# Attention with a routed feed-forward: both expert layers of 12 token tiles go through lists of routed rows, and products are scattered to a row per token and choice

## The chip, the cores and the metric

The kernel runs on one core of a Trainium2 chip. The metric is device time in microseconds of one execution; lower is better. The core has a matrix engine (PE), a vector engine (DVE), a scalar engine (ACT), a general engine (POOL) and a queue engine (SP) that only starts transfers. Each engine works through its own instructions in order and waits on semaphores for the others. Ordinary transfers are started by SP; indirect ones, in which every one of 128 rows has its own address, are started by POOL.

## What is computed

```python
x = x + xattn(_layernorm(x), ctx, ctx, mask, Wq, bq, Wk, bk, Wv, bv, Wo, bo)   # x: 2 x 1024 x 256, 64 keys, 16 heads
x = x + ffn(_layernorm(x), P_w, U1, U2, U3, W1, W2, b2)

def ffn(x, P_w, U1, U2, U3, W1, W2, b2):       # 12 experts, 3 chosen for each token
    xa = xf @ P_w.T
    C1 = _route_combine_weights(xa, U1, 3, 1.0)  # softmax over the top 3, zero elsewhere
    C2 = _route_combine_weights(xa, U2, 3, 1.0)
    C3 = _route_combine_weights(xa, U3, 3, 1.0)
    h = gelu(_mixture(xf, C1, W1))               # sum over experts of C[n,e] * (W[e] @ x[n])
    return _mixture(h, C2, W2) + C3 @ b2         # W1, W2: 12 x 256 x 256
```

## The kernel before

The 2048 tokens are 16 tiles of 128. Products that need float32 precision are three passes over a high and a low part of each operand (`split_product`, L1347): for both halves of the 256 inputs that is six matmuls.

**Attention.** One loop step handles one tile on every engine, with the tiles staggered: `scores` of tile t+1, `transpose_probs` of t, `transpose_a` of t-1, `queries` of t+2, `weigh_values` of t, `output_project` of t-1, `transpose_x` of t+3 on PE. Beside it ACT (L743) and POOL (L509) split one of the 12 chunks of expert weights (a pair of experts each, six per layer) into high and low part.

**Layer 1, dense.** For tiles 0 to 13, PE multiplies the tile with all 12 experts: six pairs of 36 matmuls in all, 512 columns each (`expert_pairs`). DVE adds the products with the routing weights (L1123). The gelu follows on ACT (L784). In the same steps the next tile is routed: logits on PE, `find_top`, `combine_weights` and `rows_of` on DVE, the exponentials as a power on POOL (L574). For tiles 0 to 11 (`S = 12`) ACT then scales h with each of its three layer 2 weights (L792), and POOL writes the three scaled tiles to DRAM with indirect transfers (`send_h`, L595): each row goes to a place in the list of its expert.

**Layer 2, by lists.** The 12 lists are cut into 47 blocks of 128 rows (`BLOCKS`), each of one expert. SP loads a block (`load_block`, L418), PE transposes it (L1649), ACT and DVE split it (L832, L1277), PE multiplies it with its expert's weights, six matmuls of 256 columns, ACT copies the product out (L840) and SP writes it to DRAM (L432). Buffers are rings: 8 loaded blocks, 3 transposed ones, 4 pairs of products. After the last block POOL fetches the three rows of every token with 36 indirect transfers (`fetch_y`, L605), and DVE adds them to x (L1302).

**The dense rest.** Tile 12's layer 2, tiles 14 and 15 in layer 1 and tiles 13 to 15 in layer 2 are dense products (six slots of 36 matmuls), beside which the fetches run. Every order is written out by hand; there is no scheduler.

```python
            def fetch_y(i):

                t, k = FETCH_ORDER[i]
                if i >= FETCHES:
                    pool.wait_ge(y_summed, i - FETCHES + 1)
                if i > AHEAD:
                    pool.wait_ge(pair_done, PAIRS * slot2(S) + i - AHEAD)
                pool.indirect_dma_start(out=y_fetched[i % FETCHES], out_offset=None, in_=y_rows[:, :],
                                        in_offset=bass.IndirectOffsetOnAxis(y_row[:, t, k:k + 1], 0)
                                        ).then_inc(y_back[i % FETCHES], 16)
```

## Time and profile before

| | us |
|---|---|
| Median of 3 timed runs | 366.2 (364.51 to 367.71) |
| Span of the profiled execution | 374.3 |
| PE busy in it | 340.8 (91%) |
| DVE busy | 285.7 (76%) |
| POOL busy | 189.6 (51%) |
| ACT busy | 181.8 (49%) |

The profiled execution gives no other time of its own than its span, which is 8.1 us longer than the median of the timed runs. Busy times of PE count overlapping matmuls generously. The share of an engine over the span says little here, since the program is a row of stages with different limits; the stages have to be read one by one.

### The profile page before, as it was taken

Reading aid. Unit: us, or ns where it says so; the run is one execution under the profiler, and the core shown is the slowest. Engines: PE = TensorE matmul, PEld = TensorE weight load, DVE = VectorE, ACT = ScalarE, POOL = GpSimd, SP = SyncE. Lnnn points to the kernel's source line nnn. Section 1 sums busy time; section 2 is a strip of 40 time slices with the busy share of each in tenths; the row PEclk is TensorE's granted clock in tenths of the full one; section 3 lists DMA queues with packets and bytes.
Section 4 is the critical chain, followed back from the end, with each engine's and each line's share of the span. In section 5 each row is a group of like instructions: output and inputs, shape, how many; then the busy total and the mean of one; then the engine's idle time right before and its main releaser. Section 6 shows DMA issues by size and latency. Waiting matters only on the chain.

```text
span 374.3 us, 7464 instructions
## 1 busy us (share of the span) xinstructions
PE 340.8 (91%) x2079; PEld 293.8 (79%) x2079; DVE 285.7 (76%) x941; ACT 181.8 (49%) x447; POOL 189.6 (51%) x263
## 2 busy tenths in 40 slices
PE   3879999999998979999999999989979899997990
PEld 3669898898998858887888888779969898885770
DVE  3899889898978568988888888886535438748757
ACT  2386978888893153344444444326747660211100
POOL 4447465655755046776666666511201017857760
PEclk9999999999999999999999999999989999998796
DMA  7910113132100001111111111556757742442442
GB/s 209 365 41 4 56 57 109 61 86 82 56 2 15 3 0 42 45 42 42 45 42 45 43 45 43 187 180 185 227 186 242 221 155 82 122 120 71 129 112 98
DMA packets 27129, 36.43 MB, mean 97 GB/s; under 512 B 3572, under 2 KB 21208, under 8 KB 26968
## 3 DMA queue, kind: packets, MB, share of 16 engines
q1 hardware_dynamic: 23080, 26.47, 22.2%
q0 software_dynamic: 3456, 9.44, 8.4%
q8 instruction: 15, 0.25, 0.3%
q10 hardware_dynamic: 560, 0.13, 0.2%
q14 instruction: 18, 0.15, 0.1%
HBM read 21.35 MB, written 14.68 MB: 96 GB/s over the span
## 4 chain that ended last, share of the span: by engine, by line
PE 65%; issue 11%; DVE 9%; ACT 6%; POOL 4%; DMA 3%; SPq 0%; ACTq 0%; DVEq 0%; POOLq 0%
PE banks L1347 48%; DMA stage<-h_rows 2%; PE banks L1649 2%; PE banks L1389 2%; PE banks L1414 2%; PE banks L1399 2%; DVE q_hl L923 2%; PE banks L1402 1%; PE banks L1404 1%; PE banks L1424 1%; ACT w_h L743 1%; PE banks L1473 1%; POOL w_l L509 1%; ACT prob L674 1%; DMA x_all<-in_x_dram 1%
## 5 line engine op out<-in xcount | busy, mean ns | idle before, releaser
L1123 DVE SCALAR_TENSOR_TENSOR sum<-banks,mask_all,sum 128x256 f32<-128x256 f32 x160 | 68.2, 477 | 16.3 <-PE banks L1347 8.2
L1347 PE MATMUL banks<-w_h,h_h 128*128 128x512 f32 x120 | 50.5, 421 | 1.4 <-DVE h_l L1054 1.4
L574 POOL TENSOR_TENSOR top_e<-euler,top_d 128x9 f32<-128x9 f32 x16 | 29.1, 1820 | 38.7 <-DVE top_d L1066 38.7
L1347 PE MATMUL banks<-w_h,xf_h 128*128 128x512 f32 x120 | 48.6, 405 | 0.0
L1347 PE MATMUL banks<-w_l,h_h 128*128 128x512 f32 x120 | 48.0, 400 | 0.0
L1347 PE MATMUL banks<-w_h,h_l 128*128 128x512 f32 x120 | 47.9, 399 | 0.0
L1347 PE MATMUL banks<-w_l,xf_h 128*128 128x512 f32 x120 | 47.0, 392 | 0.0
L1347 PE MATMUL banks<-w_h,xf_l 128*128 128x512 f32 x120 | 46.8, 390 | 0.0
L509 POOL TENSOR_TENSOR w_l<-stage,w_h 128x1024 f32 (+1 forms) x12 | 28.7, 2395 | 31.9 <-ACT w_h L743 31.9
L605 POOL DMA_INDIRECT stage<-y_rows,mask_all x36 | 35.9, 997 | 14.9 <-issue 8.9
L1277 DVE TENSOR_TENSOR kbd_l<-banks,kbd_hh 128x256 fp32r<-128x256 f32 x47 | 19.7, 423 | 23.4 <-ACT kbd_hh L832 23.1
L784 ACT ACTIVATE xn_t<-xn 128x256 f32<-128x256 f32 x16 | 6.7, 417 | 58.0 <-DVE xn L1128 52.8
L1347 PE MATMUL banks<-w_h,kbd_hh 128*128 x94 | 31.1, 331 | 0.5 <-DVE kbd_l L1277 0.5
L1424 PE MATMUL banks<-v_ext,prob_t 128*128 128x34 f32 x256 | 30.0, 273 | 0.0
L1424 PEld LDWEIGHTS banks<-v_ext,prob_t 128*128 128x128 f32 x256 | 29.9, 192 | 0.1
L1123 DVE SCALAR_TENSOR_TENSOR s_d<-banks,mask_all,s_d 128x256 f32<-128x256 f32 x40 | 17.1, 477 | 15.2 <-PE banks L1347 13.1
L595 POOL DMA_INDIRECT h_rows<-prob_t,mask_all x24 | 24.9, 1037 | 6.0 <-issue 6.0
L1347 PEld LDWEIGHTS banks<-w_h,h_h 128*128 128x128 f32 x120 | 23.3, 194 | 5.6 <-DVE h_l L1054 1.6
L1347 PEld LDWEIGHTS banks<-w_l,h_h 128*128 128x128 f32 x120 | 23.2, 194 | 5.4
L1347 PE MATMUL banks<-w_h,kbd_l 128*128 x94 | 26.9, 286 | 0.0
L1347 PE MATMUL banks<-w_l,kbd_hh 128*128 x94 | 26.8, 285 | 0.0
L1347 PEld LDWEIGHTS banks<-w_l,xf_h 128*128 128x128 f32 x120 | 22.5, 188 | 5.3 <-issue 0.3
(194 smaller groups left out, 890.3 us busy)
## 6 DMA issues: line engine op xcount, KB each, us to landing
stage<-in_w_t_dram SPq DMA_DIRECT2D x12, 512.0 KB, 3.7
stage<-h_rows SPq DMA_DIRECT2D x47, 128.0 KB, 2.7
y_rows<-prob SPq DMA_DIRECT2D x12, 256.0 KB, 2.8
y_rows<-stage SPq DMA_DIRECT2D x11, 256.0 KB, 2.9
out_dram<-x_all SPq DMA_DIRECT2D x16, 128.0 KB
h_rows<-wo_sb SPq DMA_DIRECT2D x13, 128.0 KB, 1.7
x_all<-in_x_dram SPq DMA_DIRECT2D x1, 1024.0 KB, 7.8
x_all<-in_x_dram SPq DMA_DIRECT2D x1, 768.0 KB, 7.8
```

Of the source, the lines that this page charges most:

```text
L509: pool.tensor_tensor(w_l[:, n, :, :], stage[:, slot, :, :], w_h[:, n, :, :].bitcast(F32), ALU.subtract).then_inc(w_split, 1)
L574: pool.tensor_tensor(top_e[:, :], euler[:, :], top_d[:, :, :].rearrange("p r k -> p (r k)"), ALU.pow).then_inc(e_ready, 1)
L595: pool.indirect_dma_start(out=h_rows[:, :], out_offset=bass.IndirectOffsetOnAxis(h_row[:, t, k:k + 1], 0), in_=h_w[t % 2][k], in_offset=No ...
L605: pool.indirect_dma_start(out=y_fetched[i % FETCHES], out_offset=None, in_=y_rows[:, :], in_offset=bass.IndirectOffsetOnAxis(y_row[:, t, k ...
L923: ins = dve.tensor_tensor(q_hl[other, :, group, :], q[r, :, :], q_hl[r, :, group, :].bitcast(F32), ALU.subtract)
L1123: dve.scalar_tensor_tensor(out=sums[e % 2][:, :], in0=product, scalar=weights[:, e:e + 1], in1=sums[e % 2][:, :], op0=ALU.mult, op1=ALU.ad ...
L1277: dve.tensor_tensor(bt_l[j % HT], banks[:, j % HT, 0:D].rearrange("p (c t) -> p c t", c=C), bt_h[j % HT].bitcast(F32), ALU.subtract).then_ ...
L1347: ins = pe.matmul(dst, a(c), b(c), start=(i == 0), stop=(i == len(terms) - 1))
L1389: ins = pe.matmul(ps_q[:, m, :], wq_sb[:, c, m * P:(m + 1) * P], xn_t[:, c, :], start=(c == 0), stop=(c == C - 1))
L1399: pe.matmul(banks[:, c, :].rearrange("p (h k) -> p h k", k=KEYS), ident_b[:, :], mask_bias[:, t, :].unsqueeze(1).to_broadcast([P, HPC, KEY ...
L1414: ins = pe.transpose(ps_pt[:, j, :], prob[:, 2 * j:2 * j + 2, :].rearrange("p h k -> p (h k)"), ident[:, :])
L1424: ins = pe.matmul(ps_v[:, j * 2 * VW:(j + 1) * 2 * VW], prob_t[:, j, :], v_ext[:, b, j, :], start=True, stop=True)
```

## The change

S stays 12, but for those tiles both expert layers now go by lists.

- Attention is unrolled (`for t in range(1, T + 1)`). Its steps now also hold, for earlier tiles, the second normalisation (`stats2`, `inverse_deviation2`, `normalise2`), `transpose_xf`, `copy_xf`, `logits`, `copy_z`, and for tiles 0 to 11 layer 1's routing in four groups of 4, 4, 2 and 2 tiles. `normalise2` writes the tile three times (once for each choice) into rows of 272 values: 256 of x, then the number of the row of the token and choice (`AT`), then the weight (`GATE`). Eight of the 12 weight chunks are split there, the last four in the next stage.
- POOL writes these rows to the lists with 36 indirect transfers (`send_x`), from step 10 on.
- Layer 1 of tiles 0 to 11 is 47 blocks. ACT scales the product with the weight that came with the row, and POOL scatters it with an indirect transfer to the row of its token and choice (`send_block`), instead of an ordinary store by SP. Layer 2's routing lies in this stage.
- Then come four dense slots (layer 1 of tiles 12 to 15) and a fifth (layer 2 of tile 12). Beside them SP loads three adjacent rows for each token, DVE adds them (`sum_rows`), ACT takes the gelu into three copies (`gelu_rows`), and POOL sends them to the second lists (`send_h`, 36 indirect transfers).
- Layer 2 of tiles 0 to 11 is 47 blocks again, each with a `send_block`; then three dense slots, beside which the rows are loaded and added to x (`sum_tail`). The 36 gathers of before are gone, and so are POOL's powers: ACT takes exponentials.
- Rings: 14 loaded blocks, 3 transposed, 8 products; 4 tiles of summed rows, 4 of gelu rows (`HS`).

```diff
-            def fetch_y(i):
-
-                t, k = FETCH_ORDER[i]
...
+            def send_x(t, n):
+
+                pool.wait_ge(row_set[0], RANKS[0].index(n) + 1)
+                pool.wait_ge(xf_ready, t + 1)
+                pool.wait_ge(xs_set, 12 if t < XS else 3 + t)
+                for k in range(TOP_K):
+                    pool.indirect_dma_start(out=list_rows[0][:, :],
+                                            out_offset=bass.IndirectOffsetOnAxis(row_at[0][:, t, k:k + 1], 0),
+                                            in_=xs(t)[:, k, :], in_offset=None
+                                            ).then_inc(x_sent_first if t < 2 else x_sent, 16)
...
+            def send_block(g):
+                pool.wait_ge(block_out, g + 1)
+                pool.indirect_dma_start(out=y_token[g // BLOCKS][:, :],
+                                        out_offset=bass.IndirectOffsetOnAxis(
+                                            block_in[g % LOADS][:, AT:AT + 1].bitcast(I32), 0),
+                                        in_=y_out[g % OUTS], in_offset=None,
+                                        bounds_check=TOKEN_ROWS - 1, oob_is_err=False).then_inc(y_sent[g % OUTS], 16)
+
+            for g in range(BLOCKS):
+                send_block(g)
+
+            def place_h(t):
+
+                if t >= HS:
+                    pool.wait_ge(h_sent[t % HS], 16 * TOP_K * (t // HS))
+                elif t == 0:
+                    pool.wait_ge(w_split_late, CHUNKS - EARLY)
+                if t < HS:
+                    pool.memset(hs_rows[t][:, :, GATE + 1:ROW_W], 0.0)
+                pool.iota(hs_rows[t % HS][:, :, AT:AT + 1].bitcast(I32), pattern=[[1, TOP_K], [0, 1]],
+                          base=t * TOP_K * P, channel_multiplier=TOP_K).then_inc(at_set, 1)
...
+            for t in range(HS):
+                place_h(t)
+            for t in range(S):
+                if t >= HS:
+                    place_h(t)
+                send_h(t)
+            for g in range(BLOCKS, 2 * BLOCKS):
+                send_block(g)
...
+            def block_copy(g):
+                act.wait_ge(block_done, g + 1)
+                if g >= OUTS:
+                    act.wait_ge(y_sent[g % OUTS], 16 * (g // OUTS))
+                nc.scalar.activation(y_out[g % OUTS], banks[:, Y_BANK[g % HT], 0:D], ACT.Copy,
+                                     scale=block_in[g % LOADS][:, GATE:GATE + 1]).then_inc(block_out, 1)
...
+            def gelu_rows(t):
+                act.wait_ge(h_summed, t + 1)
+                act.wait_ge(at_set, t + 1)
+                hs = hs_rows[t % HS]
+                nc.scalar.activation(hs[:, :, GATE], w_s[:, t, :], ACT.Copy)
+                nc.scalar.activation(hs[:, :, 0:D], sum_in[t % SUM_LOADS][:, 0:D].unsqueeze(1)
+                                     .to_broadcast([P, TOP_K, D]), ACT.Gelu).then_inc(hs_ready, 1)
```

On PE, in the loop of the attention before, between the scores of tile t+1 and the output projection of tile t-1, there stand:

```order
L1414 MATMUL banks<-ident,prob 128x128 x8
L1431 REGISTER_ALU
L1435 MATMUL banks<-ident,a_n 128x128 x2
L1384 REGISTER_ALU
L1386 REGISTER_ALU
L1389 MATMUL banks<-xn_t,wq_sb 128x128 x4
```

and in the changed kernel, from step 4 on (`xs` holds a normalised tile, `xf_t` its transpose, `router_w` the routing weights):

```order
L1592 MATMUL banks<-ident,prob 128x128 x8
L1617 MATMUL banks<-ident,a_n 128x128 x2
L1649 MATMUL banks<-router_w,xf_t 128x36 x2
L1635 MATMUL banks<-ident,xs 128x128 x2
L1567 MATMUL banks<-xn_t,wq_sb 128x128 x4
```

The logits of one tile and the transposes of another have moved into the step. On POOL, the end of the attention and the start of the first blocks in the changed kernel (`list_rows` are the lists, `y_token` the scattered products, `late_rows` the loaded blocks):

```order
L528 TENSOR_TENSOR var_eps<-mean_var,eps 128x1 [waits stats2_ready]
L532 TENSOR_TENSOR rstd<-var_eps,minus_half 128x1 [waits xf_ready,var2_ready]
L534 TENSOR_SCALAR shift<-mean_var,rstd 128x1 [waits rstd2_ready]
L600 DMA list_rows<-xs,mask_all 20096x272 [waits xs_set,xf_ready,row_set0]
L600 DMA list_rows<-xs,mask_all 20096x272 x2
L600 DMA list_rows<-xs,mask_all 20096x272 [waits xs_set,xf_ready,row_set0]
L600 DMA list_rows<-xs,mask_all 20096x272 x2
L663 DMA y_token<-prob,late_rows 4608x256 [waits block_out] x4
L663 DMA y_token<-prob_t,late_rows 4608x256 [waits block_out] x4
```

The sends of tiles 10 and 11 are POOL's last work ahead of the blocks, and each block then has one indirect transfer on POOL. On POOL beside the dense slots, from the fifth tile on:

```order
L680 IOTA stage 128x3 [waits h_sent0]
L689 DMA list_rows<-stage,mask_all 20096x272 [waits at_set,hs_ready,row_set1]
L689 DMA list_rows<-stage,mask_all 20096x272 x2
L680 IOTA stage 128x3 [waits h_sent1]
L689 DMA list_rows<-stage,mask_all 20096x272 [waits at_set,hs_ready,row_set1]
L689 DMA list_rows<-stage,mask_all 20096x272 x2
```

and on ACT at the same place (`sum_0`, `sum_1` take the first pair of a dense slot):

```order
L921 ACTIVATE sum_0<-banks,mask_all 128x256 [waits route,pair_done,acc]
L921 ACTIVATE sum_1<-banks,mask_all 128x256
L928 ACTIVATE stage<-mask_all 128x3 [waits at_set,h_summed]
L929 ACTIVATE stage<-late_rows 128x3x256
L910 ACTIVATE xd<-banks 128x256 [waits ht_done]
```

The numbering instruction of tile t stands on POOL behind the sends of tile t-1, and ACT's gelu of tile t waits for it (`at_set`); the gelu in turn stands in ACT's order ahead of work for the dense slots.

## Rows read from the trace of the kernel before

**Rows 1.** Stages: us; busy of each engine (instructions), PE's granted clock, DMA share, GB/s

```profile
28.00:112.00 84.00, 82.03 (x663) 75.81 (x661) 73.95 (x156) 69.94 (x144) 50.01 (x53) 1.00 0.19 57
112.00:139.00 27.00, 23.60 (x143) 19.96 (x143) 18.89 (x78) 10.02 (x24) 8.95 (x23) 1.00 0.02 6
139.00:239.00 100.00, 99.77 (x486) 80.60 (x484) 87.67 (x407) 40.89 (x109) 65.83 (x76) 1.00 0.14 50
252.00:305.00 53.00, 48.77 (x400) 47.80 (x398) 27.14 (x80) 35.13 (x108) 7.42 (x30) 0.97 0.67 209
305.00:360.00 55.00, 52.09 (x226) 41.92 (x226) 38.79 (x118) 8.74 (x25) 38.74 (x43) 0.94 0.37 104
```

**Rows 2.** Chain of work that ended last: start, us, what

```profile
...
283.95 0.22 PE banks L1649 x2
284.17 0.71 PE banks L1347 x6
...
289.96 5.58 DMA stage<-h_rows
...
344.02 7.24 PE banks L1347 x18
...
351.59 4.12 PE banks L1347 x18
...
371.47 0.43 DVE x_all L1154
```

**Rows 3.** Timeline of DVE, attention steps: start, us, line, op

```profile
28.37 1.23 DVE L929 TENSOR_REDUCE s_max<-banks 128x16 f32<-128x1024 f32 x1
...
60.47 1.22 DVE L929 TENSOR_REDUCE s_max<-banks 128x16 f32<-128x1024 f32 x1 [0.31 <-PE banks L1404]
...
66.80 1.22 DVE L929 TENSOR_REDUCE s_max<-banks 128x16 f32<-128x1024 f32 x1 [0.28 <-PE banks L1404]
...
112.36 1.19 DVE L929 TENSOR_REDUCE s_max<-banks 128x16 f32<-128x1024 f32 x1
```

**Rows 4.** Groups of ACT, whole span: line, op, count, busy, mean ns, idle before

```profile
L674 ACT ACTIVATE prob<-s_d 128x1024 f32<-128x1024 f32 x16 | 16.7, 1044 | 1.9 <-DVE s_d L935 1.9
L815 ACT ACTIVATE xf<-x_all,shift,rstd 128x256 f32<-128x256 f32 x14 | 8.4, 601 | 17.7 <-POOL shift L499 17.7
L784 ACT ACTIVATE xn_t<-xn 128x256 f32<-128x256 f32 x16 | 6.7, 417 | 58.0 <-DVE xn L1128 52.8 <-DVE sum L1123 5.2
L784 ACT ACT_TABLE_LOAD x1 | 1.3, 1283 | 0.0
```

**Rows 5.** Groups of DVE, whole span

```profile
L1123 DVE SCALAR_TENSOR_TENSOR sum<-banks,mask_all,sum 128x256 f32<-128x256 f32 x160 | 68.2, 477 | 16.3 <-PE banks L1347 8.2 <-ACT sum L801 4.0 <-issue 3.1
L888 DVE BATCH_NORM_STATS2 bn<-x_all 128x6 f32<-128x256 f32 (+1 forms) x32 | 13.4, 420 | 4.8 <-DMA x_all<-in_x_dram 4.8
L1302 DVE TENSOR_TENSOR x_all<-x_all,stage 128x256 f32<-128x256 f32 x36 | 13.1, 419 | 0.4 <-DMA stage<-y_rows,mask_all 0.3
L1094 DVE TENSOR_TENSOR w_at_e<-at_e,mask_all 128x108 f32<-128x108 f32 x16 | 4.4, 272 | 0.1
```

**Rows 6.** Timeline of POOL, the last two sends at the end of layer 1

```profile
237.83 0.96 POOL L595 DMA_INDIRECT h_rows<-s_d,mask_all  x1 [0.30 <-issue]
239.10 0.96 POOL L595 DMA_INDIRECT h_rows<-s_d,mask_all  x1 [0.30 <-issue]
```

**Rows 7.** Groups of POOL, whole span

```profile
L605 POOL DMA_INDIRECT stage<-y_rows,mask_all x36 | 35.9, 997 | 14.9 <-issue 8.9 <-DMA y_rows<-stage 3.0 <-PE banks L1347 1.8
...
L496 POOL TENSOR_TENSOR rstd<-var_eps,minus_half 128x1 f32<-128x1 f32 x16 | 9.3, 578 | 1.3
```

**Rows 8.** DMA issues by line: KB each, us from issue to landing

```profile
stage<-in_w_t_dram SPq DMA_DIRECT2D x12, 512.0 KB, 3.7
stage<-h_rows SPq DMA_DIRECT2D x47, 128.0 KB, 2.7
...
h_rows<-wo_sb SPq DMA_DIRECT2D x13, 128.0 KB, 1.7
```

More of the change, by code:

```diff
@@ L364, in xattn_ffn_kernel, with rings, tail_count @@
         w_dram = [w.rearrange("(c p) e o -> p c (e o)", c=C) for w in (w1_t, w2_t)]
+        def rings(first, last, i, ring):
+            return len([n for n in range(first, last) if n % ring == i])
+        def tail_count(t):
+            return 16 * (rings(0, 2 * BLOCKS, t % TAIL_LOADS, LOADS) + t // TAIL_LOADS + 1)
         block = ctx.enter_context(nc.Block())
@@ L447, in _ @@
+            for slot in range(DENSE, 2 * DENSE):
+                sp.wait_ge(acc, SUMS * slot + SUMS)
+                sp.wait_ge(y_added, T)
+                store(SLOTS[slot][1])
             sp.wait_ge(stored, 16 * T)
@@ new lines, in first_pair @@
+            def first_pair(slot):
+                layer, t = SLOTS[slot]
+                sums = sum2 if layer else [s[:, :] for s in sum1]
+                if slot > 0:
+                    act.wait_ge(acc, SUMS * slot)
+                act.wait_ge(pair_done, PAIRS * slot + 1)
+                act.wait_ge(route, STEPS * (8 + layer))
+                for e in range(2):
+                    nc.scalar.activation(sums[e], banks[:, BANK[0], e * D:(e + 1) * D], ACT.Copy,
+                                         scale=c_d[:, layer, t - S, e:e + 1]).then_inc(acc, 1)
@@ L884, in _ @@
+            for slot in range(AFTER, 2 * DENSE):
+                first_pair(slot)
         @block.vector
@@ new lines, in choose @@
+            def choose(n):
+                r, first, count = ROUTE[n]
+                dve.wait_ge(route, STEPS * n + PLACED)
+                i = RANKS[r].index(n)
+                if i > 0:
+                    dve.wait_ge(rank_done[r], i)
+                with nc.allow_low_precision(reason="zeros and ones"):
+                    dve.tensor_reduce(picked[r][:, 0:count, :], at_e[:, 0:count, :, :], AX_X, ALU.add).then_inc(route, 1)
+                dve.wait_ge(route, STEPS * n + CHOSEN)
+                with nc.allow_low_precision(reason="whole numbers up to 4"):
+                    dve.tensor_reduce(more[:, :], picked[r][:, 0:count, :].rearrange("p t e -> p e t"), AX_X,
+                                      ALU.add).then_inc(route, 1)
@@ L1115, in sum_pair @@
+            def sum_pair(slot, pair):
+                layer, t = SLOTS[slot]
+                sums = sum2 if layer else [s[:, :] for s in sum1]
+                weights = c_d[:, layer, t - S, :]
                 dve.wait_ge(pair_done, PAIRS * slot + pair + 1)
@@ new lines, in sum_pairs @@
+            def sum_pairs(slot, pairs):
+                for pair in pairs:
+                    sum_pair(slot, pair)
+                    if pair == PAIRS - 1:
+                        last_sum(slot)
+            sum_pairs(0, range(1, 4))
+            sum_rows(0)
+            sum_pairs(0, range(4, PAIRS))
+            sum_rows(1)
+            sum_pairs(1, range(1, 3))
+            h_low(0)
+            sum_rows(2)
+            sum_pairs(1, range(3, 5))
+            sum_rows(3)
+            sum_pairs(1, range(5, PAIRS))
@@ L1499, in expert_pairs @@
-            def expert_pairs(slot, pairs, left, layer):
-                for pair in pairs:
-                    if slot > 0:
-                        pe.wait_ge(acc, SUMS * slot - SUMS + 2 * pair + 2)
-                    n = layer * PAIRS + pair
-                    split_product(banks[:, BANK[pair], :], left,
-                                  (lambda c: w_h[:, n, c, :], lambda c: w_l[:, n, c, :])).then_inc(pair_done, 1)
-            def xf_parts(t):
-                return [whole(part) for part in xf_buffers(t)]
@@ L1674, in _ @@
+            pe.wait_ge(table[0], TABLE)
             transpose_block(0)
@@ L1718, in _, with expert_pairs @@
-            experts(S + 1)
-            experts(S + 2, ahead=False)
-            expert_bias(T - 1)
-            pe.wait_ge(h_lo, T - S)
-            expert_pairs(slot2(T - 1), range(PAIRS), h_parts(T - 1), 1)
+                if j in (6, 11, 16):
+                    rank(3 + j // 5)
+                if j == 17:
+                    row_ends(1)
+                if j == 21:
+                    transpose_table(1)
+            def expert_pairs(slot, pairs):
+                layer, t = SLOTS[slot]
+                left = [whole(part[t - S]) for part in (xd_h, xd_l)]
+                for pair in pairs:
+                    if slot not in (0, AFTER):
+                        pe.wait_ge(acc, SUMS * slot - SUMS + 2 * pair + 2)
+                    n = layer * PAIRS + pair
+                    split_product(banks[:, BANK[pair], :], left,
+                                  (lambda c: w_h[:, n, c, :], lambda c: w_l[:, n, c, :])).then_inc(pair_done, 1)
```

1759 lines of the change are left out of this document (914 added, 845 removed).

## The prediction

> **What bounds the kernel now.** I read the stages first, since each has its own limit [rows 1]. From 28 to 112 us, the attention, PE (82.0 of 84), DVE (74.0) and ACT (69.9) are all nearly full, and only POOL has room (50.0). From 139 to 239 us, dense layer 1, PE is busy for 99.8 of 100 us: matmuls are the limit, and nothing else. From 252 to 305 us the 47 blocks of layer 2 run at PE's pace, with DMA at 0.67. From 305 to 360 us PE works through dense slots again. The chain of waits [rows 2] shows the same: pieces of six or more matmuls follow each other, broken by a slow block load (5.58 us at 289.96) and by one stretch at a low clock (18 matmuls in 7.24 us at 344.02, against 4.12 us for 18 at 351.59). So PE's matmuls set the end for some 250 us, and a change that takes matmuls away can pay. POOL, at 51% of the span, looks harmless; whether it stays so is the question here.
>
> **What is removed.** Twelve dense tiles of layer 1, 36 matmuls of 512 columns each. At 4.12 us for 18 [rows 2] a tile is 8.2 us, twelve are 99 us, and with the logits and transposes between them they are most of the 139 to 239 stage. What comes for them on PE is a second set of 47 blocks: a block's six matmuls take 0.71 us (284.17) behind transposes from 283.95 on, 0.93 us in all [rows 2], so 44 us. By PE's account alone the kernel would lose some 55 us. All else in the sum is against that.
>
> **The attention.** Steps are 6.33 us apart (60.47 to 66.80); step 1 begins at 28.37 and step 14 at 112.36 [rows 3]. What the steps take in:
> ACT: `normalise2` for 768 values, between 0.6 us (256 values with scale and bias) and 1.04 (1024 values) [rows 4], I take 1.0; two copies, 0.5 together. ACT had 69.9 of 84 us, 5.3 us a step; 6.8 with these, and it must wait once for PE's queries, which stand behind logits and transposes now. I take 7.3 us for steps 2 to 9, which also split weights, and 6.9 behind them.
> DVE: `stats2`, 0.42 us for the statistics [rows 5] and 0.24 for the rest, on 5.6 us, so 6.3 to 6.7. In addition the routing groups: some 20 small instructions of 0.1 to 0.3 us (the largest form of before, 0.27 us [rows 5]), 3.6 us for four tiles, in steps 7 to 9 and 11 to 13. Steps 8 and 12 become 8.9 us.
> The loop's branch is gone, which gives back about 0.2 us a step. Summed: step 2 at 35, step 8 at 79, step 10 at 95.5, step 13 at 119, against 106 before. The attention costs some 13 us more.
>
> **The sends at its end.** This is the first term on POOL. An indirect transfer of 128 rows keeps POOL for 0.96 us, and the next starts 1.27 us after it (237.83, 239.10) [rows 6]; the 36 gathers had a mean of 1.0 us busy [rows 7], and the same gaps. Nothing in these rows was waiting for data. So an indirect transfer costs 1.26 us of POOL. `row_set` for tiles 4 to 7 comes in step 13, at 119 + 4 = 123 us. Behind it POOL has 24 sends, 30.3 us, and four second normalisations of 1.15 us (the power alone 0.58 [rows 7]): done at 158.5, while PE, DVE and ACT would be through at about 145. Landing takes 2 us (an ordinary write of 128 KB to the lists took 1.7 [rows 8]), the first block's load 2.7 and its issue 0.5, and transposes, split, product and copy 3.3 us at PE's low clock: POOL's first `send_block` is at 167 us.
>
> **The first 47 blocks.** PE needs 0.93 us a block, ACT and DVE less than that even with the routing and four weight chunks. POOL needs 1.26. In the kernel before SP stored the products, so this cost is new: 47 x 1.26 = 59 us instead of 44. The rings (8 products, 14 loads) only let PE run ahead by a few blocks. I add 2 us for the cold start and get 228 us for POOL's last send.
>
> **The dense slots and the second sends.** SP loads summed rows only when the last send has landed: 2 us, then 384 KB in about 3.5 (512 KB took 3.7 [rows 8]), two additions of 0.42 [rows 5], ACT's table load of 1.3 [rows 4], a gelu of 768 values with the weights, 1.0: the first send is 9 us behind. Four tiles are ready ahead of POOL, 4 x 3.85 = 15.4 us. From the fifth on POOL numbers the rows of tile t only behind the sends of t-1, and ACT's gelu waits for this number: POOL then stands for 1.4 us in each tile, 5.3 us a tile, eight tiles 42.4. Together 66.9 us, where five dense slots on PE are 41. The cover is too short, and it even tears: ACT waits in order for `at_set`, and with it the gelu and the first pair of slots 2 and 3, so PE will stand some 10 us in the fourth slot. That costs nothing more, since POOL is later still. Then 2 us to land, 3.2 to load and 3.2 to the first product: the first send of the second blocks is 75 us behind the last of the first, at 303.
>
> **The second blocks and the tail.** Again 2 + 59, so POOL's last send is at 364. SP loads rows 2 us later, 5.5 us until the first has landed. DVE by then has done three pairs of the first of three dense slots; left are 12 pairs at about 0.89 (0.48 an instruction [rows 5], a little overlapped), three closings of 0.85 and 12 tiles with two additions, 0.88 each: 23.8 us. The last store needs 2.4 us (374.3 less 371.47 + 0.43, where DVE ends now [rows 2]). The end is 364 + 5.5 + 23.8 + 2.4 = 396 us, 21.4 us over 374.3. The timed median lies 8.1 us below the profiled span, and I leave that distance as it is: 366.2 + 21.4 = **388 us**. POOL is in this chain from 123 to 364 us: 154 indirect transfers are 194 us of these 241.
>
> **A rule against this.** By the Trainium skill, page "DMA: Bandwidth & Descriptors", section "Anatomy of one DMA — SWDGE (gpsimd) path", descriptor generation is small, and a DMA's fixed 2 us are mostly the receipt of the write; so POOL would be free at once. By it my 154 transfers would leave the chain nearly whole, and PE would set the pace (rival 1, worked out below from rows). The trace does not agree: 0.96 us busy each, 1.27 apart.
>
> **Rivals.**
> 1. POOL doesn't set the pace. If the 0.30 us between transfers belongs to their addresses or queue and doesn't come back in `send_block`, a transfer costs 0.96 us, as PE needs for a block. All 154 transfers then save 46 us: 342. Against it: the gap stands between nearly all of the 72 of before, 8.9 us in 30 of the 36 gathers [rows 7]. For it: no scatter with a bounds check was seen. If even that cost were hidden, PE's stages would give 326.
> 2. The chain is shorter than I sum, at places where I took waits in full: gelus ready earlier in the eight tiles (11 us), attention steps at 6.7 us (5 us), no cold starts (4 us). All three give 368, about the time of before; two of them 372.
> 3. Slower still: the bounds check, or rows of 1088 bytes instead of 1024, makes a transfer 1.5 us. Over 94 or more transfers that is 23 us: 411. Also slow loads as at 289.96 could come, but 14 buffers cover 5.6 us.
> The forecast lies on the slower side; rival 1 is the one on the other. It decides from 1.11 us a transfer on: (388 - 366) / 154 = 0.14 us less than 1.26.
>
> **How the numbers follow.** Forecast, 376 to 402 us: 0.58. Rival 1: 0.17. Rival 2, from 358 to 375: 0.12. Rival 3: 0.13. A measurement of this kernel can tell about 1% (3.7 us) from no change. Faster by more: rival 1 and 0.05 of rival 2, 0.22. Within 1%: 0.07. Slower: 0.71. The range is 350 to 404: the forecast, rival 2, the upper part of rival 1 and a little of rival 3. It leaves out the low part of rival 1 and most of rival 3, 0.2 together.
>
> **What the changed profile would show.** `send_block` 1.25 us apart with POOL near full from 167 to 228 and from 303 to 364 us, and PE idle about a quarter of each block; the idle time of ACT's `block_copy` released by the landing of sends. POOL's last `send_x` 10 us or more behind PE's last `output_project`. Beside the dense slots `gelu_rows` waiting for the numbering instruction, eight times. Step 13 of the attention at 119. The forecast is wrong if transfers on POOL stand less than 1.1 us apart, or if the 66.9 us of the second sends come out near the 41 us of PE's slots.

## The result and the profile after

| | before | after |
|---|---|---|
| median of the runs, us | 366.95 (4 runs, 364.51 to 368.64) | 417.67 (4 runs, 417.05 to 418.19) |
| span of the profiled execution, us | 374.3 | 415.2 |

The ratio is 1.1414, with a 95% interval of 1.1351 to 1.1477. The changed kernel is slower by 50.7 us. The forecast was 388 us; its sign was right and its size was not. The time lies outside the range. Two of the four executions of one kernel below, `three_moves`, were longer as a whole at a lower granted clock (393.49 and 395.53 us), and its times are those of the other two.

The stages of the changed kernel answer to [rows 1]. The columns are the same: busy time and instructions of PE, its weight loads, DVE, ACT and POOL, then PE's granted clock and the DMA share.

```profile
140.00:160.00 20.00, 12.26 (x53) 10.23 (x52) 8.69 (x39) 3.62 (x11) 14.27 (x20) 0.50 0.36 126
180.00:200.00 20.00, 14.06 (x104) 12.91 (x105) 12.43 (x65) 11.35 (x28) 11.42 (x12) 0.91 0.65 207
200.00:220.00 20.00, 15.80 (x114) 14.57 (x113) 12.58 (x68) 11.71 (x32) 12.66 (x13) 0.91 0.48 144
220.00:243.00 23.00, 19.96 (x141) 18.39 (x140) 9.22 (x21) 11.22 (x29) 17.82 (x18) 1.00 0.57 184
300.00:320.00 20.00, 4.76 (x20) 4.03 (x21) 4.58 (x24) 3.83 (x9) 6.19 (x9) 0.50 0.41 126
320.00:384.00 64.00, 56.40 (x423) 52.65 (x422) 32.91 (x135) 40.85 (x120) 46.31 (x47) 1.00 0.49 154
```

POOL issues almost without a break in two of these. In the second block stage (320 to 384) it has 47 transfers and 46.3 us busy, and with the 0.30 us behind each that is 60 of the stage's 62 us. From 220 to 243 it is the same, 18 transfers. From 180 to 220, where the forecast has POOL full too, it sends 25 transfers in 40 us where 31 fit. PE is busy for 56.4 of the second stage's 64 us, where the forecast had it idle for a quarter of each block.

POOL's groups answer to [rows 6] and [rows 7] (line, output and inputs, count, busy us, mean ns, idle time ahead and what ended it):

```profile
L663 POOL DMA_INDIRECT y_token<-prob,late_rows x48 | 47.6, 992 | 28.6 <-ACT prob L879 17.1 <-issue 10.9 <-ACT prob_t L879 0.6
L663 POOL DMA_INDIRECT y_token<-prob_t,late_rows x46 | 46.2, 1004 | 30.3 <-issue 20.4 <-ACT prob_t L879 8.4 <-ACT prob L879 1.5
L600 POOL DMA_INDIRECT list_rows<-xs,mask_all x36 | 35.6, 990 | 12.4 <-issue 10.9 <-DVE mask_all L1138 1.5
```

A `send_block` costs what a gather cost: about 1.0 us busy, and 0.30 us to the next. POOL's timeline shows where the terms of the sum fall (start, us): the last `send_x`, the first `send_block`, two late ones of the first stage, the last one of it, the first `send_h`, the wait ahead of the fifth tile, the last block's send.

```profile
161.07 0.96 POOL L600 DMA_INDIRECT list_rows<-xs,mask_all  x1 [0.30 <-issue]
172.72 1.00 POOL L663 DMA_INDIRECT y_token<-prob,late_rows  x1 [10.69 <-ACT prob L879]
...
191.82 0.98 POOL L663 DMA_INDIRECT y_token<-prob_t,late_rows  x1 [2.13 <-ACT prob_t L879]
...
207.66 0.98 POOL L663 DMA_INDIRECT y_token<-prob_t,late_rows  x1 [2.87 <-ACT prob_t L879]
...
242.27 0.98 POOL L663 DMA_INDIRECT y_token<-prob_t,late_rows  x1 [0.30 <-issue]
...
251.75 1.00 POOL L689 DMA_INDIRECT list_rows<-stage,mask_all  x1 [7.76 <-issue]
...
268.63 1.15 POOL L689 DMA_INDIRECT list_rows<-stage,mask_all  x1 [1.80 <-ACT stage L929]
...
381.80 0.98 POOL L663 DMA_INDIRECT y_token<-prob_t,late_rows  x1 [0.30 <-issue]
```

The attention's steps answer to [rows 3]. Steps 8 and 10 start at 78.75 and 97.73 us, where 79 and 95.5 were expected:

```profile
78.75 1.19 DVE L1028 TENSOR_REDUCE s_max<-banks 128x16 f32<-128x1024 f32 x1
...
97.73 1.23 DVE L1028 TENSOR_REDUCE s_max<-banks 128x16 f32<-128x1024 f32 x1 [1.49 <-PE banks L1582]
```

The chain of waits in the first block stage (start, us, what) is where the forecast fails:

```profile
175.36 0.73 PE banks L1523 x6
...
176.49 0.21 ACT top_e L794
...
177.55 0.23 DVE more L1122
177.79 0.34 DVE bt L1340
...
183.46 5.84 DMA late_rows<-list_rows
...
190.96 1.28 PE banks L1523 x6
```

POOL does not appear here. Layer 2's routing stands in DVE's program between two `block_low`: its first part waits for ACT's exponentials, and `bt` (the low half of the transposed block) waits for all of it, and PE for `bt`. Once a load comes late, too, behind the weights on SP's queue. After the wait for the load six matmuls take 1.28 us and not 0.72 (granted clock 0.80 from 188 to 192 us), and again at 205.10 us, behind a row of small steps on DVE (0.57 from 204 to 208 us). The first ones behind a routing step take 0.97 us at a clock of 1.00 (178.25 us); there the price is the pause. Only from 211 us on do POOL's transfers follow each other without a break, and only from 230 us on does ACT's copy of a product wait for earlier products to land, which the forecast expected of the whole stage. ACT's copies, two late ones of the first stage and the first and the last of the second:

```profile
228.98 0.47 ACT L879 ACTIVATE prob<-banks,late_rows 128x256 f32<-128x256 f32 x1 [0.18 <-PE banks L1523]
230.04 0.48 ACT L879 ACTIVATE prob<-banks,late_rows 128x256 f32<-128x256 f32 x1 [0.31 <-DMA y_token<-prob,late_rows]
...
318.58 0.47 ACT L879 ACTIVATE prob_t<-banks,late_rows 128x256 f32<-128x256 f32 x1 [1.12 <-PE banks L1523]
...
375.69 0.47 ACT L879 ACTIVATE prob_t<-banks,late_rows 128x256 f32<-128x256 f32 x1 [1.19 <-DMA y_token<-prob_t,late_rows]
```

In both stages together ACT stood 4.8 us for landings, in five copies of the first and in the last one of the second. The second stage's copies start over 57.1 us, 1.24 us a block, while POOL takes 1.29. So there POOL is a little slower than the other engines and ends some 6 us behind them; it doesn't hold them back, and the chain that ended last runs through PE, ACT and DVE from 316 to 374 us.

### The profile page after: what moved, and what is told of

The parts are those of the page before. It is cut to its first block, busy times and chain, and to the rows that moved or that the text cites. A ratio compares the mean times of both kernels' runs of the same rounds, so it can differ in the third digit from the quotient of the medians.

```text
span 415.2 us, 7627 instructions
## 1 busy us (share of the span) xinstructions
PE 314.1 (76%) x2031; PEld 275.8 (66%) x2031; DVE 249.4 (60%) x824; ACT 207.5 (50%) x507; POOL 251.6 (61%) x349
## 4 chain that ended last, share of the span: by engine, by line
PE 29%; POOL 19%; DVE 17%; issue 17%; DMA 9%; ACT 7%; SPq 1%; ACTq 0%; POOLq 0%; DVEq 0%
PE banks L1523 15%; POOL list_rows L689 7%; POOL list_rows L600 5%; PE banks L1772 4%; DMA late_rows<-list_rows 2%; POOL y_token L663 2%; DMA y_token<-prob_t,late_rows 2%; POOL w_l L544 2%; DVE q_hl L1022 2%; DVE s_max L1028 1%; PE banks L1577 1%; DVE bt L1340 1%; PE banks L1592 1%; PE banks L1567 1%; ACT stage L929 1%
## 5 line engine op out<-in xcount | busy, mean ns | idle before, releaser
L1523 PE MATMUL banks<-w_h,bt 128*128 x376 | 83.4, 315 | 11.8 <-DVE bt L1340 11.8
L1523 PEld LDWEIGHTS banks<-w_h,bt 128*128 128x128 f32 x376 | 60.9, 201 | 16.1 <-issue 15.5
L1523 PE MATMUL banks<-w_h,xd 128*128 128x512 f32 x192 | 63.5, 413 | 6.2 <-ACT prob_t L879 4.6
L663 POOL DMA_INDIRECT y_token<-prob,late_rows x48 | 47.6, 992 | 28.6 <-ACT prob L879 17.1
L1772 PE MATMUL banks<-ident,late_rows 128*128 128x128 f32 x188 | 39.2, 295 | 33.8 <-DMA late_rows<-list_rows 21.8
L663 POOL DMA_INDIRECT y_token<-prob_t,late_rows x46 | 46.2, 1004 | 30.3 <-issue 20.4
L1340 DVE TENSOR_TENSOR bt<-banks,bt 128x256 fp32r<-128x256 f32 x94 | 38.8, 418 | 39.5 <-ACT bt L873 39.5
L1523 PE MATMUL banks<-w_l,bt 128*128 x188 | 54.9, 292 | 0.0
L600 POOL DMA_INDIRECT list_rows<-xs,mask_all x36 | 35.6, 990 | 12.4 <-issue 10.9
L1523 PE MATMUL banks<-w_l,xd 128*128 128x512 f32 x96 | 39.1, 408 | 0.0
L1402 DVE SCALAR_TENSOR_TENSOR sum<-banks,mask_all,sum 128x256 f32<-128x256 f32 x40 | 16.9, 477 | 16.7 <-PE banks L1523 9.8
```

The source lines that it names most:

```text
L600: pool.indirect_dma_start(out=list_rows[0][:, :], out_offset=bass.IndirectOffsetOnAxis(row_at[0][:, t, k:k + 1], 0), in_=xs(t)[:, k, :], i ...
L663: pool.indirect_dma_start(out=y_token[g // BLOCKS][:, :], out_offset=bass.IndirectOffsetOnAxis(block_in[g % LOADS][:, AT:AT + 1].bitcast(I ...
L1340: dve.tensor_tensor(bt_l[g % HT], halves(banks[:, g % HT, 0:D]), bt_h[g % HT].bitcast(F32), ALU.subtract).then_inc(block_lo, 1)
L1402: dve.scalar_tensor_tensor(out=sums[e % 2], in0=product, scalar=weights[:, e:e + 1], in1=sums[e % 2], op0=ALU.mult, op1=ALU.add).then_inc( ...
L1523: ins = pe.matmul(dst, a(c), b(c), start=(i == 0), stop=(i == len(terms) - 1))
L1772: ins = pe.transpose(banks[:, g % HT, c * P:(c + 1) * P], block_in[g % LOADS][:, c * P:(c + 1) * P], ident[:, :])
```

## The experiments

Times are medians. "After" is 417.7 us.

**The kernel before, once more.** The forecast was made against a profiled execution 8.1 us longer than the median.

> The kernel before, unchanged, profiled a second time. Theory A: the first profiled execution of it was about 8 to 9 us longer than the timed ones, since the changed kernel's profiled execution (span 415.2 us) took 417.05 us of device time, 1.9 us more than its span and as much as its other runs. Then this span is 363 to 367 us, and the 8 to 9 us are missing in one place, the stretch between 328 and 351 us, where the first profile showed a granted clock of 0.62. Theory B (the prediction's): profiling lengthens a run of this kernel, so the span is again 372 to 376 us with the same low clock there.

Measured: 368.37 us with a span of 366.6 us, so 1.8 us lie outside the span, and this profiled execution is no longer than the timed runs beside it (366.84 to 368.75 us). Two stretches (columns as above), first of this run, then of the first profile:

```profile
328.00:342.00 14.00, 14.00 (x65) 11.54 (x64) 11.99 (x44) 1.27 (x4) 11.37 (x11) 1.00 0.38 104
342.00:352.00 10.00, 10.00 (x47) 8.07 (x46) 9.78 (x27) 2.42 (x7) 7.32 (x10) 1.00 0.47 132
```

```profile
328.00:342.00 14.00, 12.99 (x58) 10.03 (x57) 8.40 (x34) 1.67 (x6) 8.89 (x9) 1.00 0.32 88
342.00:352.00 10.00, 8.36 (x25) 6.53 (x26) 9.18 (x25) 1.77 (x6) 7.61 (x10) 0.66 0.45 123
```

From 328 to 352 us PE does 110 instructions here and 83 there (the two rows of this run count two matmuls at their border twice), with a break and then a clock of 0.66. 27 matmuls at 0.23 us are 6.2 of the 7.7 us between the spans. The first profile had caught a hitch that the second one doesn't have. Theory A holds; what caused the hitch is open.

**Row numbers earlier** (`early_places`).

```diff
             for t in range(S):
-                if t >= HS:
-                    place_h(t)
+                if HS <= t + 2 < S:
+                    place_h(t + 2)
                 send_h(t)
```

> Only the row numbers of the gelu rows (place_h) are written two tiles earlier in POOL's program, ahead of the sends of tile t-2; four buffers stay. Theory A: from the fifth tile on POOL idles 1.80 us ahead of each group of three sends, since ACT's gelu waits for at_set, which POOL writes behind the sends before it; with the places early only the 0.30 us gap is left, so eight waits of about 1.4 us go and the time falls by 10 to 13 us, to 405 to 408 us. Theory B: something else is late there (the sums on DVE, the loads on SP or PE's dense pairs), and the time falls by less than 4 us.

Measured: 405.48 us, 12.2 less; ratio to the kernel before 1.102 (1.094 to 1.110). The wait ahead of the fifth tile's first send is gone:

```profile
265.57 0.15 POOL L680 IOTA stage<- 128x3 int32 x1
265.89 0.99 POOL L689 DMA_INDIRECT list_rows<-stage,mask_all  x1 [0.18 <-issue]
```

The 36 sends take 46.6 us (249.97 to 296.60) and not 59.6 (251.75 to 311.30). Theory A holds: the wait was on the chain, and it was in the sum.

**The last weight chunk later** (`late_weights`).

```diff
-            for n in range(EARLY, CHUNKS):
+            for n in range(EARLY, CHUNKS - 1):
                 load_weights(n)
             for j in range(LOADS, BLOCKS):
+                if j == 22:
+                    load_weights(CHUNKS - 1)
                 load_block(0, j)
```

> Only SP's order in the first block stage: the load of the last weight chunk, which waits for DVE's split of chunk 8, stands ahead of block 22 and no longer ahead of block 14. Theory A: that wait held the load of block 14 until 183.46 us, it took 5.84 us, PE stood until 189.34 us and then ran six matmuls in 1.28 instead of 0.72 us, and POOL's idle time beyond its usual 0.30 us a transfer is 4 us between 188 and 199 us. With the load in time the stage falls from 70.5 to 65 to 67 us, the time by 3 to 6 us. Theory B: POOL's 1.29 us a transfer sets the stage in any case and it catches up from the eight products that are ready; the time falls by less than 1 us.

Measured: 418.74 us, no gain. The late load is gone, and the first block stage, from its first send to the end of its last, is 68.6 us and not 70.5; but this run's attention ended its sends 1.9 us later (163.96 against 162.03), an end that moves between 160 and 164 us from run to run. So the load was worth 2 us at most, not the 4 that I gave it. The chain shows why:

```profile
194.24 0.98 PE banks L1525 x6
...
195.61 0.21 ACT top_e L796
...
196.68 0.23 DVE more L1124
196.91 0.34 DVE bt L1342
197.38 0.97 PE banks L1525 x6
```

With the blocks loaded in time, the routing steps on DVE hold PE instead. Theory A falls. B's number comes true (less than 1 us), but not its reason, since POOL isn't what holds this stretch either.

**The routing in the gap** (`routing_in_gap`). The same instructions, ahead of the first block on all three engines.

```diff
-                if 2 <= j < 17:
-                    ranked_route(4 + (j - 2) // 5, (j - 2) % 5)
...
+            for n in (4, 5, 6):
+                for step in range(5):
+                    ranked_route(n, step)
             for j in range(BLOCKS):
                 block_low(j)
```

> Only the place of layer 2's routing of tiles 0 to 11 (find, index, place, weigh, choose, ranks, rows, the exponentials): all three groups stand between attention and the first block, where DVE idles 8.3 us, and no longer between blocks 2 and 16. Theory A (the routing steps delay bt on DVE, and so PE and POOL): the stage loses 3 to 5 us, the first block starts up to 3 us later, and the time falls by 0 to 4 us. Theory B (each group is a ping-pong of DVE, ACT and PE of some 5 us, longer than the gap): the first send_block starts 5 to 8 us later and the time is 2 to 6 us longer than 417.7 us.

Measured: 413.62 us, 4.1 less; ratio to before 1.124 (1.116 to 1.132). The first send of a block comes 12.0 us after the last `send_x` and not 10.7, and the stage falls by more than I had thought, from 70.5 to 63.3 us:

```profile
175.94 1.01 POOL L663 DMA_INDIRECT y_token<-prob,late_rows  x1 [11.97 <-ACT prob L881]
...
238.28 0.99 POOL L663 DMA_INDIRECT y_token<-prob_t,late_rows  x1 [0.30 <-issue]
```

That is 1.35 us a block. Its `send_x` ended 1.9 us late, like those of the run above, so the move by itself is worth some 6 us (an estimate). Theory A holds in kind, and the stage gains 7.2 us where it had 3 to 5. This is the term that the forecast left out.

**Blocks stored by SP** (`stored_blocks`). The scatter is left out; the token sums read other products.

```diff
+            def store_block(i, j):
+                g = i * BLOCKS + j
+                sp.wait_ge(block_out, g + 1)
+                sp.dma_start(y_token[i][j * P:(j + 1) * P, :], y_out[g % OUTS]).then_inc(y_sent[g % OUTS], 16)
...
-            for g in range(BLOCKS):
-                send_block(g)
+            pool.wait_ge(block_out, BLOCKS)
```

> Both block stages: SP stores each product in block order with an ordinary transfer (and issues the loads between the stores, ten blocks ahead); POOL issues none of the 94 indirect transfers. It leaves out the scatter: the token sums that follow read other products. Theory A (the recorded one, POOL's transfers set the pace of a block stage): the second stage falls from 62.1 us to the pace of PE and the loads, 1.02 us a block as in the kernel before, 46 to 50 us; the first falls by 7 to 9 us only, since up to its 24th block the routing on DVE sets it; the time is 391 to 398 us. Theory B (PE, DVE or ACT set the pace beside POOL, or SP with two transfers a block does next): the time falls by less than 10 us.

Measured (one run, as for the next two): 414.41 us, only 3.3 less. Theory A, as it was written with its numbers, falls. Part of the cause was my own order on SP: it stood for the weights' wait ahead of its first store, and its 12 fill rows (6 us) came between the last store and the sums' loads. So I took the disturbances away, in two steps.

> As stored_blocks (SP stores the products in block order, POOL sends none; the sums that follow read other products, the scatter is left out), with layer 2's routing in the gap before the first block, and SP's fill rows of the second lists (12 transfers of 0.52 us, which in stored_blocks came behind the last store and ahead of the sums' loads) between stores 28 and 29. Theory A (corrected after stored_blocks): without POOL's sends a block stage runs at what PE, ACT and DVE take, 0.93 us a block when nothing is between, and the routing between the blocks hid that in the first stage. So the first stage falls from 63.3 us (routing in the gap, POOL sending) to 45 to 50 us, the second is 57 us as in stored_blocks, and the time is 413.6 less 13 to 18 less 5, 390 to 396 us. Theory B: something beside POOL and the routing (loads, stores, SP) holds the first stage too; it stays over 55 us and the time over 400 us.

Measured: 414.61 us. SP still stopped: at the weights' load until 184.4 us, with the five stores behind it up to 188.5 us, and from 220.1 to 226.1 us at the fill rows. In both stretches no block's load was issued (PE resumed at 229.0). This run says nothing for either theory.

> As stored_routing_out, with SP's own stops taken away: the last weight chunk's load, which waits for DVE's split, stands ahead of store 14 and not ahead of store 0 (SP stood 184.4 to 188.5 us for it and for the stores behind it, the products' ring was full and ACT waited 4.89 us), and the 12 fill rows go one behind each of the stores 29 to 40 and not in a row (SP stood 6.9 us, the loads of the next blocks came late). The scatter is left out, the sums read other products. Theory A: then the first stage, 66.9 us in that run and 63.3 us with POOL sending, is 50 to 54 us (0.93 us a block, and some 8 us for the splits of the late weights, the table and two exponentials), the second 57 us; the time is 396 to 401 us, 13 to 18 us under the run with the routing in the gap alone (413.6 us), and this is all that POOL's pace costs in the two block stages. Theory B: SP with two transfers a block (1.03 us) and the order of PE and DVE hold it as POOL did: the stage stays over 58 us and the time over 405 us.

Measured: 407.05 us, 6.6 less than with POOL sending. From the first product's copy to the last, the stages are 59.3 and 58.4 us; from POOL's first send to its last with the routing in the gap they are 62.3 and 61.5. These are Theory B's numbers: without one indirect transfer a block still takes 1.27 to 1.29 us. Four steps of this run's chain between 211 and 234 us:

```profile
211.81 5.10 DMA late_rows<-list_rows
...
221.45 0.21 SPq L440
221.85 2.50 DMA late_rows<-list_rows
...
229.88 3.82 DMA y_token<-prob_t
```

In place of POOL come SP's alternation of load and store, late landings, and, further on, exponentials and bias steps between the blocks. PE's 0.93 us is what a block takes when nothing else stands between; no stage of these kernels reached it, and the kernel before took 53 us for its 47 blocks too (ACT's first copy at 253.52 us, the last at 306.49), 1.15 us a block. SP's turns are a cost of the substitute, so 6.6 us are a lower bound of what POOL's pace costs with the routing in the gap. For the changed kernel itself its own trace gives an upper bound: with no wait for landings and sends as early as their products, the last send would come some 8 us earlier in the first stage and 6 us in the second (an estimate, from ACT's copies at 228.98 and 374.02 us with the rest at 0.94 us each, against POOL's last sends at 242.27 and 381.80 us). Between these bounds the cost stays open.

**A second, half transfer** (`half_sent_twice`).

```diff
                                         bounds_check=TOKEN_ROWS - 1, oob_is_err=False).then_inc(y_sent[g % OUTS], 16)
+                pool.indirect_dma_start(out=spare[:, :],
+                                        out_offset=bass.IndirectOffsetOnAxis(
+                                            block_in[g % LOADS][0:P // 2, AT:AT + 1].bitcast(I32), 0),
+                                        in_=y_out[g % OUTS][0:P // 2, :], in_offset=None,
+                                        bounds_check=TOKEN_ROWS - 1, oob_is_err=False).then_inc(y_sent[g % OUTS], 16)
```

> Behind each of the 94 block sends POOL issues a second indirect transfer of the block's first 64 rows to a spare buffer that nothing reads. It prices a transfer. Theory A (the cost of a transfer goes with its rows): 64 rows are 0.49 us busy and 0.30 us gap, 94 of them 74 us, less up to 8 us that POOL idles in the first stage: the time is 483 to 492 us. Theory B (the cost is that of an instruction): 0.98 us busy and 0.30 us gap again, 120 us, the time is 528 to 538 us. Under both POOL is the pace of both block stages; if it were not, the time would rise by less than 50 us.

Measured: 524.38 us, 106.7 more. POOL's timeline (block send, half send, block send):

```profile
205.07 0.99 POOL L664 DMA_INDIRECT y_token<-prob_t,late_rows  x1 [0.30 <-issue]
206.36 0.91 POOL L669 DMA_INDIRECT spare<-prob_t,late_rows  x1 [0.30 <-issue]
207.58 0.99 POOL L664 DMA_INDIRECT y_token<-prob_t,late_rows  x1 [0.30 <-issue]
```

Half the rows keep POOL for 0.91 us, and with the gap 1.22 us. The 94 added ones are 114.7 us of POOL, and 106.7 of them arrive at the end; the other 8 fell into POOL's idle time in the first stage. The cost is that of the instruction (Theory B); the time is 3.6 us below B's range, since the 0.91 us busy are not 0.98. With 2.51 us of POOL a block there is no doubt that POOL sets the pace in this run, and nearly all added time goes to the end. It prices the instruction, but doesn't show that 1.29 us a block were the pace of the unchanged stages; ACT's copies and `stored_clean` show that the other engines were close behind.

**Dense slots in the gap** (`dense_in_gap`).

```diff
-    AFTER = DENSE + 1
+    AFTER = DENSE + 3
...
+            for d in (1, 2):
+                pe.wait_ge(h_lo, d + 1)
+                expert_pairs(DENSE + d, range(PAIRS))
```

(with the sums and first pairs of these slots on DVE and ACT behind the last gelu rows)

> Three of layer 2's four dense slots (not one) stand between the two block stages, beside POOL's 36 sends; one is left behind the second block stage. The second stage's first transposes wait for all sums of those slots. Theory A: PE stands idle there (in the run with the row numbers written early, for 20 us), and behind the blocks the dense pairs set the tail of 32.4 us; so two slots of 8.3 us go from the tail and cost nothing: the time falls by 12 to 16 us, to 402 to 406 us. Theory B: the loads, sums and stores of the 12 tiles set the tail next, or the two slots delay the gelu rows and the sends; the gain is under 6 us.

Measured: 415.80 us, 1.9 less. Theory A falls, and a gain of under 6 us, as Theory B has it, is what came: the tail is 26.1 us and not 32.4, but the second block stage starts 4.0 us later. The chain:

```profile
306.95 11.31 PE banks L1512 x36
318.26 1.88 issue
320.14 0.42 PE banks L1761 x2
```

ACT takes the first pairs of the two slots behind its last gelu rows, and these wait for the row numbers, so the last slot begins only at 307 us; its 36 matmuls then take 11.3 us, at a granted clock of 0.74, where 8.2 is usual [rows 2]. The gap that I wanted to fill was held by the coupling that `early_places` removes.

**All three** (`three_moves`).

> Row numbers two tiles early, layer 2's routing in the gap, and three of layer 2's dense slots between the block stages, together. If the three gains are of different stages they add: 12 us and 4 us, measured alone, and 12 to 16 us for the third, less up to 3 us, since the stage between the block stages is now shorter and PE's idle time there is 20 us for 16.7 us of pairs: 386 to 392 us. That is still 5% above the kernel before (367 to 368 us), as the recorded theory says: 154 transfers at 1.27 us or more are 196 us of POOL time, of which these edits take none away.

Measured: 389.3 us (387.59 and 390.96), ratio to the kernel before 1.060 (1.055 to 1.066). The gains together are 28 us, more than the 18 of the three alone; a likely reason is that the dense slots gain once the row numbers are early, but no run has these two without the third. It doesn't beat the kernel before.

**The tail on one engine** (`tail_on_dve`), on top of the three moves.

```diff
-                pool.tensor_tensor(quarter(y, 1), quarter(y, 1), quarter(y, 2), ALU.add).then_inc(y_rest, 1)
...
+                dve.tensor_tensor(quarter(y, 1), quarter(y, 1), quarter(y, 2), ALU.add).then_inc(y_rest, 1)
```

> three_moves with the last sums on DVE alone (three additions a token tile; POOL's addition y_rest is now DVE's). In three_moves the additions to x on DVE took 0.42 us when POOL was idle and up to 0.95 us while POOL added beside them, 12 tiles in 17.8 us. Theory A (DVE and POOL slow each other down when both read and write the buffer memory): three additions at 0.42 us and the gaps are 1.3 to 1.4 us a tile, 12 tiles 16 to 17 us, so moving POOL's work to DVE costs nothing and may give 1 to 2 us: 389 to 393 us against 392.2 us. Theory B (no such effect, POOL's half was a real help): the tail is 4 to 6 us longer, 396 to 398 us.

Measured: 391.30 us, ratio 1.067 (1.062 to 1.073), not to be told from `three_moves` (1.055 to 1.066). The effect shows in the changed kernel's own tail: an addition to x on DVE while POOL adds (391.35 to 392.20 us), the same addition while POOL stands, and one of DVE's sums that reads one operand from the matmuls' banks, again while POOL adds (398.78 to 399.50 us):

```profile
391.52 0.96 DVE L1490 TENSOR_TENSOR x_all<-x_all,stage 128x256 f32<-128x256 f32 x1
400.07 0.41 DVE L1490 TENSOR_TENSOR x_all<-x_all,late_rows 128x256 f32<-128x256 f32 x1
398.89 0.47 DVE L1402 SCALAR_TENSOR_TENSOR xn_t<-banks,mask_all,xn_t 128x256 f32<-128x256 f32 x1
```

The sum that reads the banks is not slowed: its mean over the kernel is 0.48 us. With POOL's additions gone (`tail_on_dve`) the group of the same additions has:

```profile
L1488 DVE TENSOR_TENSOR x_all<-x_all,late_rows 128x256 f32<-128x256 f32 x4 | 1.7, 416 | 0.0
```

Alone DVE does a tile in 1.14 us (372.0 to 384.5 for 11 tiles), under the 1.3 expected. A third of the additions came over to it, and the time did not move clear of noise; Theory B's 4 to 6 us more did not come. So POOL's help gave about as much as it cost, to some 2 us.

## Why the prediction missed

The span was to be 395.7 us and is 415.2. Term by term, in the order of the sum:

| term | expected, us | measured, us | adds to the miss |
|---|---|---|---|
| last `send_x` done | 158.5 | 162.0 | +3.5 |
| from there to the first `send_block` | 8.5 | 10.7 | +2.2 |
| first 47 blocks | 61 | 70.5 | +9.5 |
| to the end of the second sends | 66.9 | 68.1 | +1.2 |
| to the first send of the second blocks | 8.4 | 9.3 | +0.9 |
| second 47 blocks | 61 | 62.1 | +1.1 |
| tail | 31.7 | 32.4 | +0.7 |

These are 19.1 us; the terms as recorded add up to 396.0, and rounding on the way makes the difference to 395.7 and 19.5. The other 10.6 us come from the step to the timed median: I took 8.1 us off the profiled span, and the median of the changed kernel lies 2.5 us above its own. So the step to the median is the largest single part of the miss, and the first block stage the largest part of the chain.

**The step that failed first** is "PE needs 0.93 us a block, ACT and DVE less than that even with the routing". By busy time that is true: DVE has 12.4 of 20 us. It is not true by order. A routing step waits for ACT or PE in the middle of DVE's program, the next `block_low` waits behind it, and this costs PE a pause: it stands for 1.02 us ahead of the product at 178.25 us. `routing_in_gap` takes the steps out, the stage falls by 7.2 us, and of the 9.5 us only 2.3 are left. The weight load in SP's order, my first suspect, is worth 2 us or less (`late_weights`). The 0.93 us failed in the second stage too, where ACT's copies come 1.24 us apart because of exponentials and bias steps between the blocks. That the term came out at 62.1 us for 61 is luck: POOL's 1.29 us hid it. [rows 1] could have warned, with 53 us for the same 47 blocks.

**The step to the median** was the second failure. "I leave that distance as it is" treated the 8.1 us as a property of profiling. I had named the stretch at a low clock myself [rows 2]; `before_again` shows that it was a hitch of that one execution, in which PE did 27 instructions fewer between 328 and 352 us. The sum should have been set against a span near 366 us.

**The attention** was right up to step 8; step 10 came 2.2 us late, waiting for PE. The sends at its end were as priced, but the four normalisations between them were not. From the first of the last 24 sends at 124.00 us to the end of the last at 162.03 POOL takes 38.0 us, of which the sends are some 30; the normalisations have the rest, near 2 us each and not 1.15:

```profile
146.75 0.19 POOL L528 TENSOR_TENSOR var_eps<-mean_var,eps 128x1 f32<-128x1 f32 x1 [0.22 <-DVE mean_var L996]
...
148.41 1.06 POOL L600 DMA_INDIRECT list_rows<-xs,mask_all  x1 [0.47 <-issue]
```

With a start 1 us later that makes up the 3.5 us. The first product took longer after that: the load on the chain is issued at 166.2 us, 1.8 us after the last rows have landed, where the sum had 0.5, and six matmuls of the first blocks ran in 1.31 us, at a granted clock of 0.50.

**The price of a transfer**, 1.26 us, was right: 1.27 for rows to the lists, 1.29 for `send_block`, which has the bounds check. Rival 3 (1.5 us) is out, though its 411 us lay nearest of all; that is luck. **The coupling through `at_set`** was right in mechanism and size: 1.80 us of idle time in seven of eight tiles and 2.05 in the other, 0.30 of it the usual gap; and taking it away gave 12.2 us where the sum had 11 for it.

**That POOL sets the pace** is half true. The last sends of both block stages wait in its queue, and from 209 us on and in the second stage it has next to no idle time beyond its gaps. But it held the other engines for 4.8 us only, and they needed nearly as long (1.24 us a block in the second stage). The forecast of POOL near full from the first stage's start is wrong. **Rival 1's prices** (342 and 326 us) were wrong by far more than the forecast. They assume that PE's stages give 0.93 us a block once POOL is out of the way. Had a transfer cost 0.96 us, the time would have been about 385 to 396 us and not 342 (an estimate: 417.7, less 3.3, by `stored_blocks`, to 14, the upper bound above, for the two block stages, less the gap of 0.30 for the 24 and 36 transfers outside them). So the range reached down to 350 us for a case that no run comes near, and not far enough up.

**By the Trainium skill**, page "DMA: Bandwidth & Descriptors", section "Anatomy of one DMA — SWDGE (gpsimd) path", descriptor generation is small. The measurement differs: `half_sent_twice` shows 0.91 to 0.99 us on POOL for each instruction, nearly whatever the number of rows (64 or 128), and of the 114.7 us added there 106.7 reach the end.

Why the change costs 50 us in all: by the forecast's count of PE's matmuls alone it should have gained some 55. The runs give back 26 to 28 us of that loss by order alone (`tail_on_dve` and `three_moves` against after). The remaining 22 to 24 us, and the 55, lie in what the lists of layer 1 need in a row: an attention whose step 14 starts at 129.5 us and not at 112.4 [rows 3]; two transitions, of 10.7 us (162.03 to 172.72) and 8.5 us (243.25 to 251.75), in which everything waits for a last transfer, its landing and a load; 36 sends of 46.6 us that PE's dense slots no longer cover; a block stage at 1.3 us a block. These I have read from the traces and not taken out one by one.

## What to carry to other kernels

An engine's busy share in a stage says nothing of a step that waits in the middle of its program: whoever adds work to an in-order engine between two links of the chain has to ask what that work waits for, and price the pause. When a pacing resource is taken away, the next one is to be priced from its pace in a stage with all its other work, not from its shortest row. A queue that is always full is not by that the one that holds the others: whether anybody waits for it stands in the waits of the engine behind the ring. And before a sum is set against a profiled execution, that execution has to be checked against a timed run; where they differ by 2%, look for the stretch that makes the difference.

## What was not expected of the hardware

- An indirect transfer's time on POOL hardly depends on its rows: 0.91 us for 64 rows, 0.99 us for 128, and 0.30 us to the next in both cases (`half_sent_twice`).
- DVE's additions of 128x256 with both operands in the buffer memory took 0.41 us alone and up to 0.96 us while POOL added in the same stretch; a sum of DVE that reads the matmuls' banks took its usual 0.47 us. By the Trainium skill, page "SBUF — State Buffer", section "Who interferes with whom", a DVE instruction with two inputs in SBUF contends with a GpSimd instruction that reads SBUF; the trace agrees, with these numbers.
- One execution of the kernel before stood out by 7.7 us of span, through one stretch with a short break of PE and a granted clock of 0.66 behind it (342 to 352 us).
